# First attention, tiles 13 to 15: TensorE takes the upper half off the turned probabilities; first routing, stores, keys and unread products are placed anew

## The reference

```
x = x + xattn(layernorm(x), ctx, ctx)   # 16 heads of 8, biases, softmax
x = x + ffn0(layernorm(x))   # 8 experts, top 2, silu(x Wg) * (x Wu) Wd, width 176
x = x + xattn(layernorm(x), ctx, ctx)   # own weights
x = x + ffn1(layernorm(x))   # 8 experts, top 2, gelu(x W1 + b1) W2 + b2, width 512
```

## Time and profile before

| | |
|---|---|
| three runs | 429.47, 430.56, 435.54 us, median 430.56 |
| profiled execution | 428.84 us, span 427.0 us |
| mean granted TensorE clock | 0.955 of 2.4 GHz |
| busy share PE / DVE / ACT / POOL | 85 / 80 / 63 / 58% |

### The profile page before, as it was taken

The page is one execution under the profiler, slowest core; times in us unless marked ns, Lnnn a source line. Parts: engine busy times, 40 slices in busy tenths (PEclk is TensorE's granted clock), DMA queues, the critical chain, the costliest instruction groups (busy, mean ns, idle before and its releaser), DMA issues.

```text
span 427.0 us, 12926 instructions
## 1 busy us (share of the span) xinstructions
PE 365.1 (85%) x4528; PEld 256.8 (60%) x4528; DVE 341.2 (80%) x978; ACT 268.8 (63%) x591; POOL 245.7 (58%) x362
## 2 busy tenths in 40 slices
PE   3977799998779999999998799898878899999900
PEld 2644566666446656666655567676634798888800
DVE  6876589998888787887876689988877899999707
ACT  3664588987457555666556788786722766767504
POOL 7860367777525558576661244456787356677630
PEclk9996899999999999999999999998996999999965
DMA  7358797000001111101002400001113223232136
GB/s 202 83 166 257 218 382 266 4 3 2 2 0 51 51 52 49 48 16 40 0 11 34 62 3 2 5 21 34 40 47 102 78 79 95 78 90 65 45 103 223
DMA packets 30837, 33.15 MB, mean 78 GB/s; under 512 B 3908, under 2 KB 22606, under 8 KB 30776
## 3 DMA queue, kind: packets, MB, share of 16 engines
q1 hardware_dynamic: 27164, 25.84, 21.2%
q0 software_dynamic: 2496, 5.18, 3.6%
q10 hardware_dynamic: 1116, 1.31, 1.0%
HBM read 15.22 MB, written 15.01 MB: 71 GB/s over the span
## 4 chain that ended last, share of the span: by engine, by line
PE 48%; DVE 17%; SPq 10%; issue 10%; POOL 9%; ACT 3%; DMA 2%; POOLq 0%; DVEq 0%; ACTq 0%
PE ps L1433 10%; PE ps L1435 9%; PE ps L1434 9%; SPq L353 5%; PE ps L1681 4%; PE ps L1529 3%; DVE area L1026 3%; POOL sorted_rows L783 3%; POOL area L819 2%; PE ps L1602 2%; PE ps L1815 1%; SPq L371 1%; POOL expert_sums L839 1%; PE ps L1835 1%; PE ps L1443 1%
## 5 line engine op out<-in xcount | busy, mean ns | idle before, releaser
L819 POOL TENSOR_TENSOR area<-area 128x512 f16<-128x512 f32 x44 | 51.0, 1159 | 41.8 <-ACT area L587 41.8
L839 POOL DMA_INDIRECT expert_sums<-area x46 | 49.7, 1081 | 27.1 <-ACT area L609 14.4
L1433 PE MATMUL ps<-w,area 128*128 128x128 f16 (+1 forms) x360 | 63.7, 219 | 0.3 <-POOL area L819 0.2
L1434 PE MATMUL ps<-w,area 128*128 128x128 f16 (+1 forms) x360 | 63.7, 219 | 0.0
L1435 PE MATMUL ps<-w,area 128*128 128x128 f16 (+1 forms) x360 | 63.7, 219 | 0.0
L1433 PE MATMUL ps<-area,w 128*128 128x512 f16 (+1 forms) x180 | 58.8, 327 | 3.1 <-DVE area L1349 1.4
L1434 PE MATMUL ps<-area,w 128*128 128x512 f16 (+1 forms) x180 | 58.5, 325 | 0.0
L1435 PE MATMUL ps<-area,w 128*128 128x512 f16 (+1 forms) x180 | 58.4, 325 | 0.0
L1026 DVE TENSOR_REDUCE area<-ps 128x8 f32<-128x512 f32 x64 | 41.2, 686 | 14.5 <-PE ps L1681 13.2
L583 ACT ACTIVATE area<-ps 128x512 f32<-128x512 f32 x44 | 26.1, 597 | 35.1 <-PE ps L1435 34.5
L633 ACT ACTIVATE area<-ps,b_now 128x256 f32<-128x256 f32 x92 | 36.2, 477 | 12.0 <-PE ps L1435 11.9
(11 more groups left out here) (241 smaller groups left out, 1039.4 us busy)
## 6 DMA issues: line engine op xcount, KB each, us to landing
sorted_rows<-filler_rows SPq DMA_DIRECT2D x16, 528.0 KB, 6.3
w_stage<-in_L_ffn_W SPq DMA_DIRECT2D x8, 512.0 KB, 4.0
w<-sorted_rows SPq DMA_DIRECT2D x23, 132.0 KB
keys<-area SPq DMA_DIRECT2D x32, 48.0 KB
area<-in_ctx SPq DMA_DIRECT2D x4, 256.0 KB, 4.8
keys<-expert_sums SPq DMA_DIRECT2D x4, 256.0 KB, 5.4
keys<-expert_sums ACTq DMA_DIRECT2D x4, 256.0 KB, 6.2
out<-x_res SPq DMA_DIRECT2D x8, 128.0 KB, 1.9
```

Source lines behind the costliest of these rows:

```text
L819: nc.gpsimd.tensor_tensor(hid[:, n % 4, 1, :], gated[:, n % 4, :], hid[:, n % 4, 0, :], ALU.subtract).then_inc(q["lo"], 1)
L839: nc.gpsimd.indirect_dma_start(out=expert_sums, out_offset=bass.IndirectOffsetOnAxis(ap=to_row[:, j, h:h + 1], axis=0), in_=ys[j % OUTS][: ...
L1433: pe.matmul(dst, lhs[0], rhs[0], start=start, stop=False, **kw)
L1434: pe.matmul(dst, lhs[0], rhs[1], start=False, stop=False, **kw)
```

## The change

- `place_keys(0, 1)` goes in front of the five constant loads and the two chunk loads.
- In the first attention TensorE, not GpSimd, takes the upper half of tiles 13 to 15 (`SUB_FIRST`); `taken` and `halved` count the semaphores of either way.
- Routing parts 0 to 2: TensorE takes the high half off the bank (`take_part`), ScalarE copies the low half (`routing_low`), VectorE's `low` falls away; `rank` 1 and 2 come later in VectorE's order.
- `output_bias_rows` is cut up: ScalarE's three copies go to steps 8 to 10 of the first experts, GpSimd's subtraction, in four quarters, to steps 11 to 14.
- The stores begin in step 7, not 8, and 21 instead of 20 are out after step 16, one of them in step 16.
- In the last steps of the second attention the statistics of tile 15 come before the shift of tile 14 and the early tables. The late table is split: `tiles_left` before, the rest behind two arrivals. `shares` goes behind the loop.
- Unread products: added at the start and in steps -2 to 0 of the first attention; 9 become 4 and 5 become 8 in the last steps of the second; 7 and 4 become 3 and 3 before the second experts.

```
@@ -67,8 +67,9 @@
 SUB_FROM = 8
+SUB_FIRST = 13
 LAST = 14
-STORED = {8: 2, 9: 4, 10: 6, 11: 9, 12: 11, 13: 14, 14: 16, 15: 18, 16: 20}
+STORED = {7: 2, 8: 4, 9: 6, 10: 8, 11: 11, 12: 13, 13: 16, 14: 18, 15: 20, 16: 21}
 AHEAD = {12: 1}
@@ -287,7 +288,15 @@
-            return l == 1 and t >= SUB_FROM
+            return t >= (SUB_FIRST, SUB_FROM)[l]
+
+        def taken(l, t):
+
+            return max(t - SUB_FIRST, 0) if l == 0 else 16 - SUB_FIRST + max(t - SUB_FROM, 0)
+
+        def halved(l, t):
+
+            return min(t, SUB_FIRST) if l == 0 else SUB_FIRST + min(t, SUB_FROM)
@@ -367,6 +376,7 @@
                 sp.dma_start(w_stage0[c].rearrange("p (a b) -> p a b", b=w_in[c].shape[2]), w_in[c]).then_inc(s["ch0_in"], 16)
+            place_keys(0, 1)
             for dst, name in ((iota8, "iota8"), (expert_rows, "expert_rows"), (table, "table"), (before16, "before16"), (filler_rows, "filler")):
@@ -377,7 +387,6 @@
-            place_keys(0, 1)
             sp.wait_ge(s["init"], 16 * 5)
@@ -495,6 +504,8 @@
                                              ACT.Copy).then_inc(q["p_hi"], 1)
+                    if l == 0 and t == TILES - 1:
+                        routing_low(F[l], 2)
                     if alive(t - 1):
@@ -508,11 +519,11 @@
                     if alive(t + 1) and turned_by_pe(l, t + 1):
-                        act.wait_ge(q["p_sub"], t + 2 - SUB_FROM)
+                        act.wait_ge(q["p_sub"], taken(l, t + 2))
                         nc.scalar.activation(pT[:, (t + 1) % 2, 1, 4:8, :], ps[:, 5, :].rearrange("p (a b) -> p a b", a=4),
...
                     elif alive(t + 1):
-                        positive_wait(act, q["p_lop"], T)
+                        positive_wait(act, q["p_lop"], halved(l, t))
                         nc.scalar.activation(p_f[:, (t + 1) % 2, :], ps[:, 5, :], ACT.Copy).then_inc(q["p_f"], 1)
@@ -523,6 +534,8 @@
                         routing_high(F[l], 2)
+                        routing_low(F[l], 0)
+                        routing_low(F[l], 1)
@@ -544,6 +557,12 @@
                 nc.scalar.activation(xTa[:, 0, t0 * P:t1 * P], ps[:, part_bank[p], 0:(t1 - t0) * P], ACT.Copy).then_inc(q["xt_hi"], 1)
+
+            def routing_low(q, p):
+
+                t0, t1 = PARTS[p]
+                act.wait_ge(q["xt_sub"], p + 1)
+                nc.scalar.activation(xTa[:, 1, t0 * P:t1 * P], ps[:, part_bank[p], 0:(t1 - t0) * P], ACT.Copy).then_inc(q["xt_lo"], 1)
@@ -556,17 +575,19 @@
...
                 q = F[l]
-                output_bias_rows()
                 routing_high(q, 3)
@@ -585,6 +606,8 @@
                         nc.scalar.activation(hid[:, (n - 1) % 4, 0, :], gated[:, (n - 1) % 4, :], ACT.Copy).then_inc(q["hi"], 1)
+                    if 8 <= n <= 10:
+                        output_bias_rows(n - 8)
                     if n == 3:
@@ -783,12 +806,13 @@
-            def output_bias_rows():
-
-                pool.wait_ge(s["rs"], 2 * TILES)
+            def output_bias_rows(k):
+
+                e = slice(2 * k, 2 * k + 2)
                 pool.wait_ge(s["b2"], 34)
-                nc.gpsimd.tensor_tensor(b2_rows[32:33, :, :], b2_raw[32:33, :, :], b2_hi[32:33, :, :], ALU.subtract).then_inc(s["b2"], 1)
-                pool.wait_ge(s["b2"], 35)
+                pool.wait_ge(F[0]["lo"], 12 + k)
+                nc.gpsimd.tensor_tensor(b2_rows[32:33, e, :], b2_raw[32:33, e, :], b2_hi[32:33, e, :], ALU.subtract).then_inc(s["b2"], 1)
+                pool.wait_ge(s["b2"], 35 + k)
@@ -811,13 +835,14 @@
             attention(0)
-            output_bias_rows()
...
                                         ALU.subtract).then_inc(q["lo"], 1)
+                if 11 <= n <= 14:
+                    output_bias_rows(n - 11)
                 g, k = divmod(n - 6, STEPS0)
@@ -1002,22 +1027,14 @@
                         outputs(t - 1)
-                    if l == 0 and t == TILES - 1:
-                        low(F[l], 2)
-                    if l == 0 and t == TILES:
-                        rank(F[l], 1)
                     if alive(t + 1):
...
                         statistics(t - 2)
-                    if l == 0 and t == TILES - 2:
-                        low(F[l], 0)
-                    if l == 0 and t == TILES - 2:
-                        low(F[l], 1)
                     if l == 0 and t == TILES - 1:
...
                     if l == 0 and t == TILES:
-                        rank(F[l], 2)
+                        rank(F[l], 1)
                     if alive(t + 3):
@@ -1050,9 +1067,9 @@
                     residual(LAST + 1)
+                    statistics(LAST + 1)
                     row_shift(LAST)
                     early_tiles()
-                    statistics(LAST + 1)
                     row_shift(LAST + 1)
@@ -1062,6 +1079,7 @@
                     statistics(TILES - 1)
+                    rank(F[l], 2)
                 else:
@@ -1207,7 +1225,7 @@
-            def late_table():
+            def tiles_left():
@@ -1218,6 +1236,9 @@
                 last_tiles(left)
+
+            def late_table():
+
                 tile_experts(MT0, MT1)
@@ -1355,10 +1376,10 @@
                 dve.wait_ge(q["tbl"], 3)
-                late_table()
-                shares()
+                tiles_left()
                 arrive(0)
                 arrive(1)
+                late_table()
                 for j in range(MT):
@@ -1369,6 +1390,7 @@
                         arrive(j + 2)
+                shares()
                 dve.wait_ge(q["pr"], 4)
@@ -1498,6 +1520,8 @@
                 n = GROUPS * l + g
+                if l == 0 and g >= 2:
+                    unread_products(2, 0, 0, 512)
                 pe.wait_ge(KV["xt"], n + 1)
@@ -1515,6 +1539,7 @@
                     pe.wait_ge(s["zero"], 11)
+                    unread_products(4, 0, 0, 512)
                 pe.wait_ge(KV["q_lo"], GROUPS * (l + 1))
@@ -1570,6 +1595,10 @@
                         output_bias()
+                        pe.wait_ge(KV["v_lo"], 2 * GROUPS)
+                        unread_products(6, 5, 0, 512)
+                    if l == 0 and t == 0:
+                        unread_products(3, 6, 0, 512)
                     if l == 1:
@@ -1606,6 +1635,8 @@
                         turn_part(l, 2)
+                        take_part(l, 0)
+                        take_part(l, 1)
                     if l == 0 and t == TILES - 1:
@@ -1614,6 +1645,11 @@
                         scores(t + 3, (t + 3) % 2, 1).then_inc(q["s_ps"], 1)
+                    if l == 0 and t == -2:
+                        unread_products(2, 5, 0, 512)
+                    if l == 0 and t == -1:
+                        pe.wait_ge(s["bo"], 2)
+                        unread_products(2, 6, 0, 512)
                     if alive(t + 1) and turned_by_pe(l, t + 1):
@@ -1632,6 +1668,8 @@
                         weigh_values(t)
+                    if l == 0 and t == TILES - 2:
+                        take_part(l, 2)
@@ -1665,9 +1703,9 @@
                         turn_row(j)
-                        unread_products((1, 9, 1)[j - LAST + 1], 5, 0, 512)
+                        unread_products((1, 4, 1)[j - LAST + 1], 5, 0, 512)
                         row_logits(j)
-                    unread_products(5, 5, 0, 512)
+                    unread_products(8, 5, 0, 512)
                     part_ranks(4)
@@ -1745,8 +1783,17 @@
                         pe.wait_ge(q["xd"], t - POOL_ROWS + 1)
-                    mm = pe.transpose(ps[:, part_bank[p], (t - t0) * P:(t - t0 + 1) * P], rows_now[t // G][:, t % G * P:(t % G + 1) * P], ident[:, :])
+                    mm = pe.matmul(ps[:, part_bank[p], (t - t0) * P:(t - t0 + 1) * P], rows_now[t // G][:, t % G * P:(t % G + 1) * P], ident[:, :],
+                                   is_transpose=True, start=(t == t0), stop=(t == t1 - 1), skip_group_check=True)
                 mm.then_inc(q["xt_ps"], 1)
+
+            def take_part(l, p):
+
+                q = F[l]
+                t0, t1 = PARTS[p]
+                pe.wait_ge(q["xt_hi"], p + 1)
+                pe.matmul(ps[:, part_bank[p], 0:(t1 - t0) * P], minus_ident16, xTa[:, 0, t0 * P:t1 * P], start=False, stop=True,
+                          skip_group_check=True).then_inc(q["xt_sub"], 1)
@@ -1878,13 +1925,13 @@
                 pe.wait_ge(s["ch_lo"], PIECES + 2 * len(chunks))
-                pe.wait_ge(s["b2"], 51)
+                pe.wait_ge(s["b2"], 54)
                 experts = [pe.value_load(expert_i[0:1, 0:1], min_val=0, max_val=EXPERTS - 1)]
                 first_biases(0)
-                unread_products(7, 5, 0, 512)
+                unread_products(3, 5, 0, 512)
                 turn(0)
                 turn(1)
-                unread_products(4, 6, 0, 512)
+                unread_products(3, 6, 0, 512)
                 pe.wait_ge(q["b1"], 1)
```

19 lines of the change are left out of this document (11 added, 8 removed).

## The result

| | before | after |
|---|---|---|
| median, us | 430.01 (429.43 to 435.54, 4 runs) | 423.62 (421.89 to 425.35, 4 runs) |
| profiled execution, us | 428.84 | 421.89 |
| its span, us | 427.0 | 420.1 |
| mean granted clock | 0.955 | 0.972 |

The ratio is 0.9868, with a 95% interval of 0.9829 to 0.9907: 1.3% faster (the two medians alone would give 1.5%), within the 2% that the prediction took for its line. I had said 422.5 (418.8 to 427.2), and 421.4 for the profiled execution.

A forecast was written before the change was run, and what follows sets the result against it. No engine bounds the whole run: VectorE is full in the first attention's middle, single waits count elsewhere. −3.6 + 0.2 − 2.0 − 2.0 = −7.4 us took the profiled 428.84 to 421.4, the median to 422.5; range 418.8 to 427.2.

The forecast's parts named there:

- Start: Start of the first attention: earlier keys and full clock from unread products, −3.6 us; gain bounds 1.2 and 4.8.
- Tiles 13 to 15: First attention: TensorE replaces GpSimd's subtractions, nothing gained, and a new wait before the turned copies costs 0.2 us.
- First routing: First routing: low halves and bias subtraction leave VectorE, tile 15's row comes earlier, −2.0 us; bounds 0.9 and 3.0.
- the bias subtraction goes out of VectorE's way: First routing: VectorE's normalise of tile 15 falls from 2.24 to some 0.3 us, 1.95 us less.
- Bias in the first experts: First experts: ScalarE's three copies and GpSimd's quarters (0.53 us each) fit idle time; nothing paid, at worst 0.5 us.
- Second attention: Second attention: earlier stores cost 0.6 us (bounds 0 and 2); one store fewer before tile 15's rstd gains 1.27.
- Second experts: Start of second experts: earlier tile 15 row and fewer unread products, −2.0 us net of second attention's cost; bounds 0.5 and 3.2.
- beyond that the load at 335.88 is late: Second experts: past the 3.2 us bound the sixth load limits, since the last eight stores move only 0.65 us.
- Rival 1: Clock stays at 2.4 GHz into the second experts, keys fully hidden, routing near its bound: −10 us, 420.0; chance 0.24.
- Rival 2: Start: keys inherit the queue and fills don't hold the clock, start only −1.2; total −3.5 us, 426.5; chance 0.22.
- rival 3: Second attention: GpSimd becomes the bound, ten steps each pay 0.9 us, run slower at 432; chance 0.04.
- rival 4: First routing: the subtraction did not hold VectorE, 2.24 us stays, routing gives 0.5, run 424.0; chance 0.06.

The follow-up runs named there:

- e1: Kernel before with only the second part of the keys issued right behind the three weight loads, no products added at the start: 430.16 us, ratio 0.9988.
- e2: Kernel before with only the unread products at the start and in the first attention's first steps, keys where they were: 429.42 us, ratio 0.9973.
- e5: Kernel before with only TensorE, not GpSimd, taking the upper half off in tiles 13 to 15 of the first attention: 431.77 us, ratio 1.0026.
- e6: Kernel before with only the first routing's three low halves moved from VectorE to TensorE and ScalarE, ranks ordered as after: 429.44 us, ratio 1.0000.
- e3: Kernel after with the output-bias split back ahead of the routing, GpSimd's subtraction in one piece of 1024 elements: 423.78 us, ratio 0.9815.
- e7: Kernel after with the stores of the sorted rows back in the steps they had before, the first two in step 8: 426.69 us, ratio 0.9918.
- e9: Kernel after with TensorE's pauses in the second attention and second experts filled with extra products: 420.76 us, ratio 0.9772.
- e12: Kernel before with e2's products at the start and e9's fills in the second attention and second experts: 427.99 us, ratio 0.9966.
- e4: Kernel after with GpSimd again taking the upper half off in tiles 13 to 15 of the first attention: 420.99 us, ratio 0.9789.
- e11: Kernel after with VectorE's late table ahead of the first two arrivals, as in the kernel before: 422.96 us, ratio 0.9821.

## Why the prediction was right, step by step

The time and the range held. The profiled execution gained 6.95 us where the sum had 7.4: 3.71 by tile 5, 1.58 in the routing, 1.49 from the second attention to the last split, and 0.17 in what lies between and behind. By the parts:

- **Start, −3.6.** Measured −3.71 at tile 5. The mechanism is as e1 and e2 have it: keys and clock, each worth little alone (0.2 and 0.7 us of A). The sum made them additive (2.2 and 0.8 and 0.8), which they are not, and that it fitted is in part luck: it was made from the longer course of the start. Against e5 and e6, A is 2.9 us shorter, not 4.40.
- **Tiles 13 to 15, +0.2.** Measured +0.87. This step failed in its size: it costed the product beside the loop of the kernel before, where it is 0.26, and not in the queue that the low halves make on the same two engines.
- **First routing, −2.0.** −1.58 with the title, −2.45 without. The step that failed is "the bias subtraction goes out of VectorE's way". The row is long where it and the subtraction start together (2.24 us beside 2.12, again in e5 beside 2.11) and short where they do not, but moving the bias was worth only 0.10: the low halves and ranks had already brought the row ahead of ScalarE's last bias copy, for which the subtraction waits. By the Trainium skill, "SBUF — State Buffer", section "SBUF: two separate sides", the one that holds the shared ports keeps them for its whole instruction; the traces of the kernel before and e5 agree, since the long row ends within 0.1 us of the subtraction. In both the records have the row start first, by 0.05 and 0.04 us, so they don't show that GpSimd had the ports before it. In e3 and e6 the two don't overlap.
- **Bias in the first experts, 0.** Holds: 113.43 and 113.42 us. The quarters on GpSimd took 0.66 to 0.93 us, not 0.53, and VectorE's weight splits lost nothing that reaches the end, so the rule that I weighed against the change was not felt.
- **Second attention, +0.6 and −1.27.** The second is right (1.24 by e7); the first is within 0.2 us of nothing (58.57 against e7's 58.75; e9's 57.54 against e12's 57.45, to tile 14). GpSimd's stores bound nothing there.
- **Second experts, −2.0 with the row of tile 15.** Measured: C −0.64 and D −0.85, together −1.5; with the pauses filled −1.08 and −0.13, together −1.2. This step failed in its size: the 2.2 us for fewer products are not there. D is the place where the prediction named a limit and then did not use it: "beyond that the load at 335.88 is late". With the pauses filled the start of the experts is worth 0.13 us, since the last stores set it. Of the 0.85 the rest is a half clock in the kernel before from 324 to 331 us, beside the shorter one after.

Rival 1 came half true: the clock stayed full from 324 to 328 us, where the kernel before had it half, and then fell, behind TensorE's wait for the third tile's low half, which stands behind the late table on VectorE. Rival 2's start did not come, rival 3 was nowhere seen, and rival 4 is out by e5, e3 and e6: 2.24 us where the subtraction starts with the row, 0.35 where it does not. One reading was wrong without moving the sum: the 1.29 us of the earlier trace rows are the two maxima of a tile together, not each.

What the prediction left out is the half clock that moves: no term stood for the stretches at 270 us and 328 us in the kernel after, nor for the one at 293 us in the kernel before. They cost the kernel after 1.0 us in C (86.85 against 85.86) and some tenths in D.

## What to carry over

A fill of TensorE and an earlier transfer can each be worth under a microsecond alone and nearly three together, so run both halves before dropping one. When an operation is held by a neighbour's, ask what lets each of the two start; here half a microsecond between rstd and a copy on a third engine decided it, and the step named in the title only cost. Where the same program scatters by 1 or 2%, look for TensorE's pauses of over a microsecond and fill them before measuring anything finer, and before giving a stage's gain to an edit, look whether that stage ran at the same clock in both profiles.

## What the runs showed that I had not expected

- Half-clock stretches of 3 to 7 us, once of 13 us (e7), followed pauses of 1.4 to 2.6 us on TensorE, and not each pause brought one: behind the pause at 287 us the kernel after shows none, e4 one at 286 to 290. Nor has each stretch such a pause: e11 has one at 321 to 324 us with no pause of over a microsecond since 297 us.
- Twelve products of 256 columns with 64 rows of zeros, added into scores that were still being summed, filled a pause of 1.7 us (1.48 us of work), and no half clock followed in e9's profiled execution.
- The first attention's middle and the first experts repeat to 0.06 and 0.03 us from kernel to kernel and chip to chip; nearly all scatter comes from the start and from behind the second attention's first choosing.
- GpSimd's subtraction over one row cost 2.12 us for 1024 elements and 0.66 to 0.93 us for 256, so cutting it in four made 3.2 us of it.
